# Moving the last norm's weight, offset, gate and residual from the routed rows into the experts' stage

## The reference

```python
h = _layernorm(x) * (1 + cb) + sb
y = _layer_norm(h + _mha(h, Wqkv, bqkv, Wo, bo), g1, be1)      # attention over 16 rows, 4 heads
# _moe: each row goes to the one expert with the largest logit
idx = argmax(y @ Wg.T)
moe = relu(y @ W1[idx] + b1[idx]) @ W2[idx] + b2[idx]
z = _layer_norm(y + moe, g2, be2)                               # (v - mean) * rsqrt(var + eps) * g2 + be2
out = x + gb * z
```

## Time and profile before

| | |
|---|---|
| median of 3 runs | 1046.9 us (1046.08 to 1047.27) |
| the profiled execution | 1047.97 us, span 1046.2 us |
| PE, DVE, ACT, POOL busy | 82%, 83%, 60%, 69% of the span |
| POOL's indirect transfers to `out_dram` (L1930) | 71, 69.1 us busy, 78.6 us idle before them |
| chain that ended last | from 878.6 us on: first loads, then nearly all PE in `run_experts` |

### The profile page before, as it was taken

How to read it: one execution, slowest core, us unless ns; L and a number is a source line. 1 busy time by engine, 2 the same in 40 slices (tenths; PEclk the granted TensorE clock), 3 DMA queues, 4 the chain that set the end, 5 groups by cost and what they waited for, 6 DMA issues and landing times. The chain is left out here.

```text
span 1046.2 us, 25423 instructions
## 1 busy us (share of the span) xinstructions
PE 860.2 (82%) x5240; PEld 618.0 (59%) x5240; DVE 867.7 (83%) x2853; ACT 631.7 (60%) x1636; POOL 721.6 (69%) x626
## 2 busy tenths in 40 slices
PE   5799999999968867989898989558888732999993
PEld 5466666666636644555555555335555532999993
DVE  5589999999976976989898989778899761899995
ACT  2555555555438956676767675467665202999992
POOL 4488888888852218999999999665598461355554
PEclk9899999999989989999999999869999755999997
DMA  9520000000000000000000000254576664544420
GB/s 245 164 69 1 0 0 0 0 0 0 1 4 1 0 1 1 11 20 10 20 10 20 10 20 10 67 153 110 158 213 205 186 221 124 146 129 132 133 65 20
DMA packets 64935, 70.11 MB, mean 67 GB/s; under 512 B 8965, under 2 KB 52178, under 8 KB 64740
## 3 DMA queue, kind: packets, MB, share of 16 engines
q1 hardware_dynamic: 50612, 47.20, 16.2%
q0 software_dynamic: 6368, 16.89, 4.7%
q10 hardware_dynamic: 7872, 5.08, 1.8%
HBM read 32.32 MB, written 24.50 MB: 54 GB/s over the span
## 5 line engine op out<-in xcount | busy, mean ns | idle before, releaser
L473 PE MATMUL a_pS<-a_kv,utri 128*128 128x360 f32 (+3 forms) x768 | 264.9, 481 | 19.4 <-POOL a_kv L464 9.7
L464 POOL TENSOR_TENSOR a_kv<-a_qk,a_vv 128x1152 f32<-128x1152 f32 (+1 forms) x128 | 264.2, 2065 | 12.6 <-DVE a_qk L438 12.6
L473 PEld LDWEIGHTS a_pS<-a_kv,utri 128*128 128x128 f32 x768 | 136.3, 191 | 100.8 <-issue 25.3
L569 POOL TENSOR_TENSOR a_tt<-a_tt 128x576 f32<-128x576 f32 (+1 forms) x128 | 156.9, 1226 | 49.9 <-DVE a_tt L553 46.0
L553 DVE TENSOR_TENSOR a_tt<-a_pS,a_qk 128x360 f32<-128x360 f32 (+3 forms) x384 | 181.0, 526 | 11.3 <-PE a_pS L473 8.3
L1930 POOL DMA_INDIRECT out_dram<-x_o,x_place x71 | 69.1, 973 | 78.6 <-DVE x_o L1917 75.9
L581 DVE TENSOR_REDUCE a_nd<-a_tt 128x144 f32<-128x720 f32 (+3 forms) x128 | 104.5, 816 | 0.0
L519 ACT ACTIVATE a_tt<-a_pI 128x144 f32<-128x144 f32 (+1 forms) x96 | 40.1, 417 | 105.5 <-PE a_pI L481 105.4
L512 PEld LDWEIGHTS a_pO<-wgate,a_yT 128*128 128x128 f32 x256 | 44.8, 193 | 75.2 <-issue 36.6
L1512 POOL DMA_INDIRECT ys<-m_S,m_dest x64 | 63.0, 984 | 36.8 <-issue 12.3
L512 PE MATMUL a_pO<-wgate,a_yT 128*128 (+1 forms) x256 | 54.7, 296 | 30.8 <-POOL a_yT L543 22.6
(11 more groups left out here) (298 smaller groups left out, 2192.8 us busy)
## 6 DMA issues: line engine op xcount, KB each, us to landing
x_yl<-ys SPq DMA_DIRECT2D x71, 193.5 KB, 2.4
X<-xs SPq DMA_DIRECT2D x16, 256.0 KB, 5.4
kx<-m_kc SPq DMA_DIRECT2D x64, 64.0 KB
ax<-m_pc SPq DMA_DIRECT2D x64, 64.0 KB
m_S<-X SPq DMA_DIRECT2D x16, 256.0 KB, 3.1
xs<-X SPq DMA_DIRECT2D x15, 256.0 KB
w<-in_L_ffn_W_dram SPq DMA_DIRECT2D x1, 2048.0 KB
m_S<-gw ACTq DMA_DIRECT2D x6, 256.0 KB, 3.0
```

The lines of the kernel that those rows point to most:

```text
L464: pool.tensor_tensor(kv[:, t % 2, :, :, :], kk.unsqueeze(2).to_broadcast([P, H, J, D]), vv[:, t, :, :].unsqueeze(3).to_broadcast([P, H, J, ...
L473: pe.matmul(pS[c][:, 0:(h1 - h0) * SC], K.utri[:, :], flat[:, h0 * SC:h1 * SC], start=True, stop=True).then_inc(u_done, 1)
L569: pool.tensor_tensor(tt[:, t % 2, :, :, D // 2:D], tt[:, t % 2, :, :, D // 2:D], tt[:, t % 2, :, :, 0:D // 2], ALU.add).then_inc(half_done, 1)
```

## The change

Rows now carry x itself and the gate itself. `pool_xb` and the two products `K.gw` and `gb` go; SP's copy of x no longer waits for POOL, and ACT sends `K.tab[:, 2]` (the gate). The copy of the token numbers moves from DVE's `vec_stats` to ACT (`act_places`). In `run_experts`, DVE's two instructions use the constant rows g2 and be2, and POOL multiplies by the gate and adds x, in two new 128x128 instructions for each slot, with the scatter of the slot before between them. The output ring grows from four to six tiles, and the ring of loaded rows is released by POOL's add.

```diff
@@ attention: K.gw and its wait removed
-                    pool.tensor_tensor(K.gw[:, :], K.rows[:, 2, :], K.tab[:, 2, :], ALU.mult).then_inc(gw_ready, 1)
-                    sp.wait_ge(gw_ready, 1)
@@ attend_and_route
-        def pool_xb(pool, g):
-            pool.wait_ge(xn_ready, 4 * g + 4)
-            pool.wait_ge(gate_done, 1)
-            x = K.X[:, ds(4 * g, 4), :]
-            pool.tensor_tensor(x, x, over(gb[:, :]), ALU.add).then_inc(xb_ready, 1)
@@ vec_stats
-            v.tensor_copy(S[:, ring(g), TO], ids[:, 4 * g:4 * g + 4]).then_inc(place_done, 1)
+        def act_places(act, g):
+            if g == 0:
+                act.wait_ge(tab_in, 5 * 16)
+            if g >= RG:
+                act.wait_ge(rows_out[g % RG], 64 * (g // RG))
+            act.activation(S[:, ring(g), TO], ids[:, 4 * g:4 * g + 4], ACT.Copy).then_inc(place_done, 1)
@@ act_step, behind act_hT(s + 3) and act_stats
+            if there(s - 2):
+                act_places(act, s - 2)
@@
-                act.dma_start(S[:, ring(s), GO:], K.gw[:, :].unsqueeze(1).to_broadcast([P, 4, P])).then_inc(gate_in[s], 16)
+                act.dma_start(S[:, ring(s), GO:], K.tab[:, 2, :].unsqueeze(1).to_broadcast([P, 4, P])).then_inc(gate_in[s], 16)
@@ pool_step (both places)
-                if there(s + 3):
-                    pool_xb(pool, s + 3)
@@ sp_xb
-                    sp.wait_ge(xb_ready, g + 1)
+                    if g >= 4:
+                        sp.wait_ge(x_in[g], 16)
@@ vector, at the start of the block
-                v.tensor_tensor(gb[:, :], K.rows[:, 3, :], K.tab[:, 2, :], ALU.mult).then_inc(gate_done, 1)
@@ run_experts
-    ROWS = 20
+    ROWS, OUTS = 20, 6
@@ sp_rows
-            wait(sp, o_ready, j - ROWS + 1)
+            wait(sp, added, j - ROWS + 1)
@@ vec_tm
-            y_arrived(v, j)
-                                   in1=yl[:, j % ROWS, GO:], op0=ALU.subtract, op1=ALU.mult).then_inc(tm_ready, 1)
+                                   in1=K.rows[:, 2, :], op0=ALU.subtract, op1=ALU.mult).then_inc(tm_ready, 1)
@@ vec_o
-            if j >= 4:
-                v.wait_ge(z_out[s], 16 * r)
-            v.scalar_tensor_tensor(out=o[:, s, :], in0=tm[:, j % 2, :], scalar=rs[:, r % 2, s:s + 1],
-                                   in1=yl[:, j % ROWS, XO:GO], op0=ALU.mult, op1=ALU.add).then_inc(o_ready, 1)
+            if j >= OUTS:
+                v.wait_ge(z_out[j % OUTS], 16 * (j // OUTS))
+            v.scalar_tensor_tensor(out=o[:, j % OUTS, :], in0=tm[:, j % 2, :], scalar=rs[:, r % 2, s:s + 1],
+                                   in1=K.rows[:, 3, :], op0=ALU.mult, op1=ALU.add).then_inc(o_ready, 1)
@@
+        def pool_gate(pool, j):
+            pool.wait_ge(o_ready, j + 1)
+            y_arrived(pool, j)
+            at = o[:, j % OUTS, :]
+            pool.tensor_tensor(at, at, yl[:, j % ROWS, GO:], ALU.mult).then_inc(gated, 1)
+        def pool_add(pool, j):
+            pool.wait_ge(gated, j + 1)
+            at = o[:, j % OUTS, :]
+            pool.tensor_tensor(at, at, yl[:, j % ROWS, XO:GO], ALU.add).then_inc(added, 1)
         def pool_scatter(pool, j):
-            pool.wait_ge(o_ready, j + 1)
+            pool.wait_ge(added, j + 1)
@@ POOL's order
                     if j % 4 == 0 and j + 4 < SLOTS:
                         pool_places(pool, j // 4 + 1)
-                    pool_scatter(pool, j)
+                    pool_gate(pool, j)
+                    if j >= 1:
+                        pool_scatter(pool, j - 1)
+                    pool_add(pool, j)
+                pool_scatter(pool, SLOTS - 1)
```

More of the change, by code:

```diff
@@ L348, in attention @@
         proj_ps, x_done, bn_done, x_out = sem("proj_ps"), sem("x_done"), sem("bn_done"), sem("x_out")
-        gw_ready, x_back = sem("gw_ready"), sem("x_back")
+        x_back = sem("x_back")
         YT = P + H * J
@@ L1172, in attend_and_route @@
         o_ps, oT_ready, w_ps, u_ready, bn_done = sem("o_ps"), sem("oT_ready"), sem("w_ps"), sem("u_ready"), sem("bn_done")
-        gate_done, xb_ready, mask_ready, lg_ready = sem("gate_done"), sem("xb_ready"), sem("mask_ready"), sem("lg_ready")
+        mask_ready, lg_ready = sem("mask_ready"), sem("lg_ready")
         before, ones, steps = (sb(n, [P, P]) for n in ("before", "ones", "steps"))
@@ L1178, in attend_and_route @@
         uln, umv, pick, raw = sb("uln", [P, 8]), sb("umv", [P, 16, 2]), sb("pick", [P, 8, E]), sb("raw", [P, 16, E])
-        gb = sb("gb", [P, P])
         best, posf = sb("best", [P, 8]), sb("posf", [P, 8])
@@ L1766, in run_experts @@
         pT, pA, pB, pZ = ([pb(f"{n}{i}") for i in range(2)] for n in ("pT", "pA", "pB", "pZ"))
-        yl, yn, o = sb("yl", [P, ROWS, ROW]), sb("yn", [P, 6, P]), sb("o", [P, 4, P])
+        yl, yn, o = sb("yl", [P, ROWS, ROW]), sb("yn", [P, 6, P]), sb("o", [P, OUTS, P])
         place = sb("place", [P, SLOTS], U32)
@@ L1773, in run_experts @@
         yg_ready, yn_ready, place_ready = sem("yg_ready"), sem("yn_ready"), sem("place_ready")
-        y_in, z_out = [sem(f"y_in{s}") for s in range(ROWS)], [sem(f"z_out{s}") for s in range(4)]
+        y_in, z_out = [sem(f"y_in{s}") for s in range(ROWS)], [sem(f"z_out{s}") for s in range(OUTS)]
         y_T, yT_ready, w1_ready, h_ps, h_act, h_vec, z_ps = (
@@ L1778, in run_experts @@
             sem(n) for n in ("yb_ready", "u_ready", "bn_ready", "mv_ready", "sd_ready", "rs_ready", "tm_ready", "o_ready"))
+        gated, added = sem("gated"), sem("added")
         half = FC // 2 * P
@@ L1925, in pool_places @@
             pool.tensor_copy(place[:, 4 * r:4 * r + n], yl[:, at:at + n, TO]).then_inc(place_ready, 1)
+        def pool_gate(pool, j):
[7 more added lines that the diff above has]
+            pool.tensor_tensor(at, at, yl[:, j % ROWS, XO:GO], ALU.add).then_inc(added, 1)
         def pool_scatter(pool, j):
-            pool.wait_ge(o_ready, j + 1)
+            pool.wait_ge(added, j + 1)
             pool.wait_ge(place_ready, j // 4 + 1)
             pool.indirect_dma_start(out=token_rows, out_offset=bass.IndirectOffsetOnAxis(ap=place[:, j:j + 1], axis=0),
-                                    in_=o[:, j % 4, :], in_offset=None, bounds_check=B * T - 1, oob_is_err=False)\
-                .then_inc(z_out[j % 4], 16)
+                                    in_=o[:, j % OUTS, :], in_offset=None, bounds_check=B * T - 1, oob_is_err=False)\
+                .then_inc(z_out[j % OUTS], 16)
         with nc.Block() as block:
@@ L1940, in _ @@
                         pool_places(pool, j // 4 + 1)
-                    pool_scatter(pool, j)
-                for s in range(4):
-                    pool.wait_ge(z_out[s], 16 * ((SLOTS + 3 - s) // 4))
+                    pool_gate(pool, j)
[3 more added lines that the diff above has]
+                pool_scatter(pool, SLOTS - 1)
+                for s in range(OUTS):
+                    pool.wait_ge(z_out[s], 16 * ((SLOTS + OUTS - 1 - s) // OUTS))
             @block.sync
@@ L2068, in build @@
         K.wg8, K.cols, K.mod, K.tab = sb("wg8", [P, E]), sb("cols", [P, 10]), sb("mod", [P, 6, B]), sb("tab", [P, 3, P])
-        K.gw = sb("gw", [P, P])
         K.bo, K.rows, K.mask = sb("bo", [P, P]), sb("rows", [P, 4, P]), sb("mask", [2, P + 32])
```

## The result

The changed kernel takes 1067.62 us (median of four runs, 1066.64 to 1072.03), against 1046.49 for the kernel before in the same set of runs: a ratio of 1.0218, 95% interval 1.0192 to 1.0244. The profiled execution is the longest of the four, 1072.03 us with a span of 1070.2.

A forecast was written before the change was run, and what follows sets the result against it. DVE sets the routing step, POOL close; PE carries the experts' stage, DVE no less tight. 1047.97 - 8 + 27 + 4 = 1071.0, less 1.07 for the median: 1070 us; range 1059 to 1085 (0.55), wider 1046 to 1094.

The forecast's parts named there:

- tail: End of the experts' stage: fourth last tile to last scatter takes 9.5 us instead of 5.6, +4 us.
- POOL's own slot: Experts' stage: POOL's gate, scatter, add and share of the copy sum to 2.12 us, over the slot's 2.018.
- DVE's slot, held by POOL: Experts' stage: one POOL product free, the other delays DVE, giving 2.40 us a slot, bounds 2.12 and 2.91.
- slots, first `o` to last: Experts' stage: 71 slots, each 2.40 us instead of 2.02, add +27 us, bounds +7 and +63.
- experts' stage in all: Experts' stage: longer slots, +27 us, and a longer end, +4 us, taken together.
- routing stage: Routing stage: less DVE and POOL work, -6.5, -0.8 and -0.3, about -8 us, bounds -3 and -12.
- the 0.62 us: POOL, experts' stage: gate product's start to scatter's start, a product's 0.45 plus 0.17 us.
- Rival A: Experts' stage: POOL is the bound at 2.12 us a slot, DVE's blocking hidden; 1051 us, chance 0.20.
- the main term: Routing stage: DVE loses the token-number copies, 10.3 us in groups 0 to 10, of which 6.5 us kept.
- Rival D: Routing stage: PE's wait for transfers replaces the gain, 2 us instead of 8; chance spread over the other rivals.
- PE waiting for DVE's relu: Experts' stage sign: the new trace shows PE with waits for DVE's relu; PE idles 0.4 us a slot.
- rival A's sign: Experts' stage: DVE's mean instruction times stay and POOL has no idle time in the stage.

The follow-up runs named there:

- memsets: The changed kernel with POOL's two products a slot replaced by memsets of 128x408 into scratch tiles, and eight output tiles for six: 1064.72 us, 1.0184.
- pairs of slots: The changed kernel with one POOL gate product and one addition of 128x256 per two slots, then two scatters, and eight output tiles: 1060.52 us, 1.0142.

## Why the prediction was right, and where its steps were not

The time (1070 against 1067.6) and the sign were right. The mechanism was right in part: it named both limits, POOL's stream and DVE held by POOL's reads, and DVE is held. It made DVE alone the one that decides and put POOL's stream 0.28 us below it, while POOL's stream alone takes nearly all of the loss. That the sum came within 2.4 us is in part luck: its slots were too long by 9 us, and its tail was too short by 4 and its routing gain too large by 2.

| | forecast | measured |
|---|---|---|
| POOL's own slot | 2.12 us | 2.27 (memsets), 2.32 in the change |
| DVE's slot, held by POOL | 2.40 us | 2.32 in the change, 2.20 (pairs of slots) |
| slots, first `o` to last | +27 us | +18.3 us |
| tail | +4 us | +8.3 us |
| experts' stage in all | +31 us | +26.6 us in the profile, 1.0278 timed |
| routing stage | -8 us | -6 us timed |

**POOL's slot.** The term mis-sized was the 0.62 us from the gate product's start to the scatter's, made of a product's 0.45 and an idle time of 0.17 that the earlier trace rows shows behind products of 1.29 us. It is true in every fourth slot, the one with the copy (0.62, median of nine), and in the others it is 0.84 (median of 26). That is 0.22 x 3/4 = 0.17 us a slot. From a scatter's start to the next product it is 1.08 on average and not 1.02; the other two terms are 0.03 lower together. 2.12 + 0.17 + 0.06 - 0.03 is the 2.32. The row nearest in length was never there to read: before, no short product stands ahead of a scatter, and I should have kept a bound above for it. Rival A made POOL the bound, as the memsets bear out, and with 2.32 in place of 2.12 its sum gives 1065 where it had 1051. But its other half, that the blocking is hidden, is wrong: between 920 and 1000 us `tm` takes over 0.36 us in 31 of 34 slots and `yb` in 26 of 35.

**DVE's slot.** DVE is held as forecast, and by reads alone: with memsets of the same length `tm` is 343 ns, with products 460. The Trainium skill says the same (SBUF — State Buffer, "Who interferes with whom"): a DVE instruction with two SBUF inputs contends with a GpSimd instruction that reads SBUF, and not with one that only writes it. These two runs agree with both halves of that. What was wrong is the price: I took one of the two products as paid in full, 0.38 us a slot, and DVE lost 0.30 in the change and 0.18 with pairs of slots. The 2.40 was thus nearer to DVE's slot than the 2.12 to POOL's. It also had DVE kept from running ahead by the six output tiles; they never did that before the last tile.

**Which limit is on top.** POOL's stream with no read gives 2.27, and with pairs, where POOL has time to spare, DVE held by reads gives 2.20; in the change both engines take 2.32, and with neither limit the slot is 2.01. Setting DVE free, by memsets, gives back 0.05 us a slot and 2 to 4 us of some 21 by the times, which their intervals hardly tell from nothing. So POOL's stream alone is enough for nearly all of the loss. That DVE by itself would be below POOL is less sure: the 2.20 is that of longer products in another order, and no run has two single products a slot beside a shorter stream of POOL. That DVE, when it gets ahead of POOL, runs into POOL's reads until it is back at POOL's pace fits the constant lag and the missing waits, and is argued, not shown. So is the last 0.05 between 2.27 and 2.32: from a scatter's start to the next instruction's it is 1.08 us in the change and 1.00 with the memsets, which may be POOL waiting for DVE's reads in turn. Removing one limit uncovers the other, which is why 1064.7 and 1060.5 are all that the single cures reach.

**The tail.** I let POOL start the last three tiles with no lag. In fact a tile's scatter starts some 4.7 us behind the end of DVE's work on it in the whole steady part, since the gate product of the next slot stands ahead of it and DVE is two tiles on. And DVE's last tiles come fast, five within 4.1 us (1046.29 to 1050.39), while POOL takes 2.3 us for each: the lag grows from 4.7 to 11 us in the last five slots. From the end of the fourth last tile to the end of the last scatter, the prediction's own measure, it is 14.6 us against the 9.5 forecast and the 5.6 before.

**The routing stage.** The changed routing is worth 6 us by its timed ratio; -8 stood in the forecast, with -3 to -12 as bounds. The copy that I put down as the main term, 6.5 us, gives 2.4 to 4.7 alone by the medians of its two runs. The rest, 1 to 4 us, goes with `pool_xb`, the `gb` product and the waits on them; no run separates these. In single profiles the gain jumps: from POOL's first product to its last scatter, the ten kernels with the changed routing have 171.8 to 178.2 us (median 173.9) against 178.6 before and 177.1 in the one other profile of the old routing. A reason can be read in the profile of the change, which is the worst of them:

```profile
751.61 0.98 POOL L1510 DMA_INDIRECT ys<-m_S,m_dest  x1 [0.30 <-issue]
752.60 1.31 POOL L1243 TENSOR_TENSOR m_U<-m_xn,tab 128x512 f32<-128x512 f32 x1
752.14 1.81 DVE L1457 SCALAR_TENSOR_TENSOR m_S<-m_umv,m_S 128x8 f32<-128x8 f32 x1
```

An instruction of 128x8 on DVE, 0.17 us where it is free, now takes 1.81 and ends with POOL's product, as the copy used to. The copy is gone, but what waited behind it meets POOL's products in its place. In the two of the ten profiles that are over 177 us, the second instruction of this kind takes 1.81 and 1.60 us, in the other eight 0.14 or 0.15. That this is where the missing gain of those profiles went is a reading; no run isolates it. Rival D (PE's wait for the weights' transfer takes the gain) is borne out in part only: that wait is 17.5 us with a longest of 5.3, against 13.6, but it is 17.0 too in the kernel with the changed routing alone, whose stage is one of the short ones (172.9 us).

**What the forecast listed as signs.** The two products at 0.45 (they are 0.464 and 0.447), `bn` and `u` unchanged: right. A slot of 2.4: 2.32. PE waiting for DVE's relu: hardly. Half of rival A's sign, POOL without a wait in the stage, holds, together with the grown `tm`, which I had listed as its opposite. Both can be true at once.

By the Trainium skill (GPSIMD Engine Reference, "Engine selection") a two-input instruction is about twice slower on GpSimd; here 0.45 against 0.28 us, 1.6 times. It was neither this ratio nor the 0.91 us of products that decided, but the scatter between them and the reads beside DVE's.

## What to carry to other kernels

Work moved to a half-empty engine must be laid out as that engine's whole stream, with the dead time of each switch between kinds of instruction, before it is called room; here 0.91 us of products into 0.97 us of room made a slot 0.3 us longer. Where the moved instructions read SBUF, price the other engine's hold too, and expect two limits: a cure for one shows only the distance to the next. Look at the lag between the two engines and at the waits for free buffers too: a ring that is never full isn't what keeps them at one pace. And ask what an engine that was waiting for others lags by at the end, where the others' last pieces come fast.

## What the runs showed of the hardware

The start of an indirect transfer on POOL goes by the start of the product ahead of it, not by its end, when the product is short. From the start of the last product (or memset) to the scatter, in slots without the copy, medians of 7 to 28:

| last instruction ahead | its length | start to scatter | idle |
|---|---|---|---|
| 128x64 product | 0.34 us | 0.83 us | 0.49 us |
| 128x128 product | 0.47 | 0.84 | 0.37 |
| memset of 128x408 | 0.45 | 0.87 | 0.42 |
| memset of 128x640 (pairs) | 0.63 | 0.84 | 0.21 |
| 128x256 product (pairs) | 0.68 | 0.84 | 0.16 |
| 128x512 product | 1.29 | 1.46 | 0.17 |

So about 0.84 us, or the instruction's own length and 0.16, whichever is longer. It is no fixed time from the end of the scatter before: that is 1.25 us in the changed kernel, 1.14 with half products and 1.83 with pairs. With only one product between two scatters it is 0.77, and with the copy ahead of a short last instruction 0.62 behind a product and 0.73 behind a memset; the memset of 128x1 in the same place leaves it at 0.81. Between two scatters with nothing between them the idle time is 0.30. What POOL does in that time is not shown. It isn't the two waits that were dropped, and it isn't the product's reads, since the memsets show it as well.
